# A mixture of experts, computed densely per token before, routed into tiles sorted by expert after

## The reference, cut to what matters

```python
router_logits = x @ wg.T                      # x: layer norm of the residual, 4096 tokens x 128; 8 experts
probs = softmax(router_logits)
topk_w, topk_idx = top_k(probs, 2)
topk_w = topk_w / sum(topk_w)
expert_w = sum(one_hot(topk_idx, 8) * topk_w[..., None], axis=1)
h1 = einsum('th,eih->tei', x, w1)             # 8 experts x 256 inner columns
h3 = einsum('th,eih->tei', x, w3)
y = einsum('tei,ehi->teh', silu(h1) * h3, w2)
out = einsum('te,teh->th', expert_w, y)       # only 2 of the 8 weights of a token are not zero
```

## Time and profile before

| what | value |
|---|---|
| time, median of 3 runs | 1891.29 us (1890.69 to 1895.58) |
| profiled execution, its own time | 1891.74 us |
| its span | 1889.9 us |
| busy: PE, DVE, ACT, POOL | 1677.0, 1390.6, 1243.3, 901.2 us |
| stage A, until the first layer norm of stage B | 0 to 432.1 us |
| stage B, until the first layer norm of stage C | to 808.2 us |
| stage C, until stage D begins | to 1060.3 us |

### The profile page before, as it was taken

The page is one execution under the profiler, slowest core; times in us unless marked ns, Lnnn a source line. Parts: engine busy times, 40 slices in busy tenths (PEclk is TensorE's granted clock), DMA queues, the critical chain, the costliest instruction groups (busy, mean ns, idle before and its releaser), DMA issues.

```text
span 1889.9 us, 38285 instructions
## 1 busy us (share of the span) xinstructions
PE 1677.0 (89%) x12962; PEld 1368.8 (72%) x13024; DVE 1390.6 (74%) x2923; ACT 1243.3 (66%) x2747; POOL 901.2 (48%) x720
## 2 busy tenths in 40 slices
PE   4899999987999999979999599999959699999868
PEld 3777777766766767667777478888847588888746
DVE  6888888865888888866667478888736477777556
ACT  4888888864655555577877377777723377777622
POOL 4666666643544445510101277777700377777500
PEclk9999999998999999989999799999969899999979
DMA  5000000000000000010000000000000000000000
GB/s 203 1 0 0 0 0 0 0 1 1 1 1 1 1 0 0 1 49 1 0 0 0 6 13 15 14 14 15 12 5 1 9 15 14 14 14 14 9 15 34
DMA packets 39787, 23.27 MB, mean 12 GB/s; under 512 B 36257, under 2 KB 36641, under 8 KB 38945
## 3 DMA queue, kind: packets, MB, share of 16 engines
q1 hardware_dynamic: 39712, 22.33, 4.0%
HBM read 11.86 MB, written 2.10 MB: 7 GB/s over the span
## 4 chain that ended last, share of the span: by engine, by line
DVE 35%; ACT 25%; PE 23%; issue 11%; POOL 4%; DMA 1%; DVEq 1%; SPq 0%; POOLq 0%; ACTq 0%
ACT d_p L543 9%; ACT a_p L543 5%; DVE slot L1433 4%; DVE d_ss L1416 4%; DVE d_B L1424 4%; PE slot L367 3%; ACT c_p L543 3%; ACT d_sq L1356 3%; DVE d_A L1422 3%; PE slot L369 3%; PE slot L368 3%; PE slot L1544 2%; DVE b_gl L957 2%; PE slot L771 2%; PE slot L489 2%
## 5 line engine op out<-in xcount | busy, mean ns | idle before, releaser
L1471 POOL TENSOR_TENSOR d_r<-d_vv,nhalf 128x16 f32<-128x16 f32 x64 | 186.4, 2912 | 252.8 <-DVE d_vv L1421 252.8
L998 POOL TENSOR_TENSOR b_sp<-b_s,b_wb 128x512 f32<-128x512 f32 x128 | 170.5, 1335 | 175.3 <-ACT b_s L828 168.8
L665 POOL TENSOR_TENSOR rs<-mv,nhalf 128x1 f32 (+1 forms) x128 | 71.7, 560 | 326.3 <-DVE mv L660 326.3
L543 ACT ACTIVATE d_p<-slot,d_nm,d_r 128x128 f32<-128x128 f32 x512 | 186.0, 469 | 50.8 <-DVE d_nm L1437 50.8
L543 ACT ACTIVATE a_p<-slot,a_nm,a_rq 128x77 f32<-128x77 f32 x512 | 165.4, 454 | 26.2 <-DVE a_nm L567 26.2
L957 DVE TENSOR_TENSOR b_gl<-b_g,b_gh 128x512 fp32r<-128x512 f32 x128 | 133.0, 1039 | 42.4 <-ACT b_gh L832 41.5
L1416 DVE TENSOR_REDUCE d_ss<-d_sq 128x16 f32<-128x1024 f32 x64 | 78.1, 1220 | 109.4 <-ACT d_sq L1356 109.4
L1473 POOL TENSOR_TENSOR d_A<-d_A,d_B 128x1024 f32<-128x1024 f32 x64 | 151.3, 2364 | 0.0
L828 ACT ACTIVATE b_s<-slot 128x512 f32<-128x512 f32 x128 | 76.6, 598 | 81.6 <-PE slot L369 76.7
L543 ACT ACTIVATE c_p<-slot,c_nm 128x77 f32<-128x77 f32 x512 | 118.0, 363 | 11.7 <-DVE c_nm L1156 11.7
L1341 PE MATMUL slot<-d_v,d_pT 128*128 128x65 f32 x1024 | 124.0, 275 | 0.0
(11 more groups left out here) (269 smaller groups left out, 5166.6 us busy)
## 6 DMA issues: line engine op xcount, KB each, us to landing
X<-in_x SPq DMA_DIRECT2D x2, 1024.0 KB, 8.0
d_zx<-Z SPq DMA_DIRECT2D x64, 32.0 KB
H<-Z SPq DMA_DIRECT2D x64, 32.0 KB
out<-f_o SPq DMA_DIRECT2D x8, 256.0 KB, 2.0
d_zx<-Z SPq DMA_DIRECT2D x64, 31.8 KB
H<-Z SPq DMA_DIRECT2D x64, 31.8 KB
stage<-in_wqkv SPq DMA_DIRECT2D x2, 768.0 KB, 5.4
ctx_sb<-in_ctx SPq DMA_DIRECT2D x1, 1232.0 KB, 7.5
```

What stands on the lines that cost most here:

```text
L543: i = e.activation(t["p"][:, h, :], R[slot][:, k // nbank, nk * (k % nbank):nk * (k % nbank) + nk], ACT.Exp, bias=t["nm"][:, h:h + 1], sca ...
L998: e.tensor_tensor(t["sp"][:, c % 2, :], t["s"][:, c % 2, :], t["wb"][:, c // 2 % 2, :], ALU.mult)\
L1471: e.tensor_tensor(t["r"][:, p, :], t["vv"][:, p, :], nhalf[:, 0:16], ALU.pow).then_inc(S("d_r"), 1)
```

## The change

The mixture is computed only for the two experts that a token has. While stage A runs, each finished block is normalised (`r_xn`), its router logits are taken, the two largest are found (`max`, `max_index`), and after every fourth block a place in a list per expert is computed for each token and choice (`chosen`, `places`). POOL scatters the rows to HBM by these places (two indirect transfers of 128 rows per block), into two arrays `xs` that SP first clears (18432 rows of 512 bytes each, 9.44 MB, one of them ahead of `w1e` and `w3e` in the queue). The tokens are in two segments of 16 blocks; tables of each segment (`tables`) say for 40 tiles of 128 rows which expert a tile has. Stage B walks over 80 tiles: SP loads a tile from HBM by an address read from the table, PE transposes it, multiplies it by both weight matrices of one expert (`w13`, 3 passes of 512 columns), transposes the result and multiplies by `w2e`, and SP writes the answer to HBM. Stage C gets two lags more: POOL gathers the two answers of every token (two indirect transfers per block), DVE adds them with their weights to `X` and computes the statistics there. The rest of the diff renames and merges semaphores and passes `part` to the iterations.

The diff, cut to its core:

```diff
@@ load @@
-            for n, src in enumerate((w1e_in, w3e_in, w2e_in)):
-                e.wait_ge(S("split"), (1, 2, 4)[n])
-                e.dma_start(stage[:, n % 2, :], src).then_inc(S(f"stage{n % 2}_in"), 16)
+            nothing = zero[:].unsqueeze(1).to_broadcast([128, ZROWS // 512, 512])
+            for h in range(SEG):
+                if h == 1:
+                    for n, src in enumerate((w1e_in, w3e_in)):
+                        e.wait_ge(S("split"), n + 1)
+                        e.dma_start(stage[:, n, :], src).then_inc(S(f"stage{n}_in"), 16)
+                e.dma_start(xs[h].rearrange(...).rearrange(...), nothing).then_inc(S(f"cleared{h}"), 16)
@@ a_vector, at block b5 = it.b(5) @@
+                    layernorm(e, X, r_["xn"], b5, m).then_inc(S("r_v"), 1)
...
+                    e.tensor_copy(r_["xT"][:], R[1][:, 1, 0:128]).then_inc(S("r_v"), 1)
...
+                    e.max(r_["mx"][:, m, :], R[1][:, 1, 128:128 + NE]).then_inc(S("r_v"), 1)
+                    e.max_index(r_["ix"][:, m, :], r_["mx"][:, m, :], R[1][:, 1, 128:128 + NE]).then_inc(S("r_v"), 1)
+                    if m == 3:
+                        chosen(b5)
+                        places(b5, it.part)
@@ a_pool @@
+        def scatter(e, it, j, lag):
...
+                for k in range(2):
+                    e.indirect_dma_start(xs[it.part][:, :], bass.IndirectOffsetOnAxis(ap=r_["ps"][:, j, k:k + 1], axis=0),
+                                         r_["xn"][:, j, :], None).then_inc(S(f"r_sc{j}"), 16)
+                if it.phase > 0:
+                    scatter(e, it, it.phase - 1, 9)
+                if it.phase == 3:
+                    scatter(e, it, 3, 8)
@@ b_tensor, one tile per iteration @@
+                    e.transpose(bank(m % 2)[:, 0:128], t["x"][:, m, :], ident[:]).then_inc(S("b_T1"), 1)
...
+                    k = e.value_load(table["expert"][0:1, bass.ds(b, 1)], min_val=0, max_val=NE - 1)
...
+                    passes(e, bank(2 + q), [x[:, q, :] for x in t["xT"]],
+                           [w[:, bass.ds(k, 1), :].rearrange("p a b -> p (a b)") for w in w13]).then_inc(S("b_H"), 1)
...
+                    for c in range(2):
+                        mm = e.transpose(bank(4 + q)[:, 128 * c:128 * c + 128], t["g"][:, q, 128 * c:128 * c + 128], ident[:])
...
+                    k = e.value_load(table["expert"][0:1, bass.ds(b, 1)], min_val=0, max_val=NE - 1)
+                    for c in range(2):
+                        mm = e.matmul(bank(6 + q)[:, 0:128], t["gT"][:, q, c, :], w2e[:, bass.ds(2 * k + c, 1), :]...,
+                                      start=(c == 0), stop=(c == 1))
+            pipeline(e, SEG * NT, 4, 4, body)
@@ b_sync, on SP @@
+                    k = e.value_load(table["read"][0:1, bass.ds(b, 1)], min_val=0, max_val=NE * ROOM)
+                    if past(b - 4):
+                        e.wait_ge(S("b_T1"), count(b - 4))
+                    e.dma_start(t["x"][:, m, :], xs[it.part][bass.ds(k, 128), :]).then_inc(S(f"b_x{m}"), 16)
...
+                    e.dma_start(ys[bass.ds(b * 128, 128), :], t["y"][:, m, :]).then_inc(S(f"b_out{m}"), 16)
@@ c_vector, ahead of the maxima @@
+                    for k in range(2):
+                        e.scalar_tensor_tensor(out=rows(X, b), in0=t["yg"][:, m, k:k + 1, :], scalar=r_["w"][:, k, bass.ds(b, 1)],
+                                               in1=rows(X, b), op0=ALU.mult, op1=ALU.add).then_inc(S("c_mix"), 1)
+                    e.bn_stats(st[:, 1, :], rows(X, b)).then_inc(S("c_st"), 1)
+                    e.bn_aggr(agg[:, 1, :], st[:, 1, :]).then_inc(S("c_st"), 1)
+                    e.tensor_tensor(rows(mv, b), agg[:, 1:2, :], eps[:, 1:2, :], ALU.add).then_inc(S("c_st"), 1)
@@ c_pool @@
+                    for k in range(2):
+                        e.indirect_dma_start(c_["yg"][:, m, k, :], None, ys[:, :],
+                                             bass.IndirectOffsetOnAxis(ap=c_["gi"][:, m, k:k + 1], axis=0)).then_inc(S(f"c_g{m}"), 16)
```

More of the change, by code:

```diff
@@ L62, in upto, with pipeline, nth @@
         return last + base + 1
-def pipeline(eng, n, lags, unroll, body):
+def pipeline(eng, n, lags, unroll, body, parts=None, between=None):
     assert lags % unroll == 0 and (n - lags) % unroll == 0
+    ends = (parts or []) + [n]
     for i in range(lags):
[L69 to L72, removed]
+        body(It(i, i % unroll, n, unroll, 0))
+    for part, end in enumerate(ends):
+        first = lags if part == 0 else ends[part - 1]
+        assert (end - first) % unroll == 0
+        if part > 0 and between is not None:
+            between(part - 1)
+        with eng.Fori(first, end - unroll + 1, unroll) as r:
+            for u in range(unroll):
+                body(It(r + u, u, n, unroll, part))
     for i in range(n, n + lags):
-        body(It(i, i % unroll, n, unroll))
+        body(It(i, i % unroll, n, unroll, len(ends) - 1))
+    if between is not None:
+        between(len(ends) - 1)
 def past(b):
     return type(b) is not int or b >= 0
+def nth(n, j, k):
+    return (n - 1) * k + j
 def count(b, j=1, k=1, base=0):
@@ L252, in program @@
         f["o"] = at("f_o", [128, 2, 512])
+        xs = [nc.dram_tensor(f"routed{h}", (ZROWS, D), F32, kind="Internal").ap() for h in range(SEG)]
+        ys = nc.dram_tensor("answers", (SEG * YROWS, D), F32, kind="Internal").ap()
         made = {}
@@ L441, in body @@
                                 e.wait_ge(S("ac_pTb"), it.upto(3))
+                        if half == 1 and b5 is not None:
+                            logits(b5)
                         for k in range(4):
@@ L651, in body @@
                         e.wait_ge(S("rs"), NB // ST)
-            pipeline(e, NB, 4, 4, body)
+            pipeline(e, NB, 8, 4, body, [A_PART], tables)
+            for h in range(SEG):
+                answers(h)
+            e.wait_ge(S("r_ex"), 1)
+            e.tensor_scalar(r_["w"][:, 0, :], r_["dn"][:], 1.0, None, ALU.add).then_inc(S("r_w"), 1)
+            e.wait_ge(S("r_w"), 9)
+            e.reciprocal(r_["w"][:, 0, :], r_["w"][:, 0, :]).then_inc(S("r_w"), 1)
+            e.wait_ge(S("r_w"), 10)
+            e.tensor_tensor(r_["w"][:, 1, :], r_["dn"][:], r_["w"][:, 0, :], ALU.mult).then_inc(S("r_w"), 1)
         def stats_tail(e, b, bn, ag, vs, k=1, j=0, base=0):
@@ L1260, in da_tensor @@
             da_start(e, l)
[L1261 removed]
+            e.wait_ge(S("split"), 8)
             e.wait_ge(S("d_con"), 7)
```

918 lines of the change are left out of this document (487 added, 431 removed).

## The result

The changed kernel takes 2020.62 us (median of 4 runs, 2005.31 to 2023.89) against 1891.93 us before (4 runs, 1890.69 to 1895.58): ratio 1.066, 95% interval 1.060 to 1.072, 129 us slower. The prediction was 1875 us with a range of 1805 to 1960: the wrong side, and outside the range. The profiled execution took 2017.88 us, its span is 2015.8.

What follows compares the result with a forecast made beforehand. PE was taken to bound stage B, rings through DVE and ACT stages A and C. The terms 13 + 55 + 8 + 5 + 9 - 162 + 55 = -17 took 1891.7 to 1875 us, range 1805 to 1960.

Steps and rivals of the forecast that it cites:

- +8 us: Stage A: POOL's indirect transfers mostly hide in slack; 1 us shows in each of eight iterations with four transfers.
- The rival on POOL: POOL becomes stage A's bound at 2.92 us per indirect transfer, giving 1981 us; chance 0.10.
- estimate from the port rule: Stage A: a POOL transfer takes 0.62 us alone, 3.1 beside a VectorE copy; the latter would cost some 120 us.
- 443.9 + 90 = 534 us: Start of stage B: 443.9 us before the change, predicted at 534 with the terms 13, 55, 8, 5 and 9.
- The start's +13: Start of stage A: clearing 9.44 MB ahead of `w1e` and `w3e` in SP's queue stalls everything 13 us.
- Stage B's tile: Stage B: each of 80 tiles takes 2.4 us, bounds 2.1 to 2.8; with the end, -162 us.
- the 2.6 that was named as a sign of being wrong: Stage B: the prediction falls if a tile takes over 2.6 us, where the gain of 17 is used up.
- The term for PE's own work, 1.6: Stage B: PE's transposes, three wide products and two float32 products take 1.6 us per tile.
- The term for the reads, 0.8 for both: Stage B: two table reads at 0.6 us each, partly hidden, between a tile's products on PE.
- reads on the path: Stage B: reads of 0.9 us, PE's sequencer unable to run ahead; tile 3.4 us, kernel 1955; chance 0.19.
- The rival of the low clock: Stage B: at 1.2 GHz PE's 1.6 us becomes 3.1, the tile about 3.3, the kernel 1947; chance 0.08.
- The ring through the maxima: Stage C: maxima, ACT, `c_qTl` and DVE's list form a ring; 1.65 us a block ahead of the maxima adds 55.

Runs made afterwards that it cites:

- e1_xn8: The changed kernel with eight buffers in place of four for `r_xn` and `r_ps`, stage A's loops unrolled by eight: 1918.72 us.
- e7_split: Eight buffers as in e1_xn8, with the second block's two scatters moved behind `a_kn` in POOL's list: 1887.92 us.
- e4_early: The changed kernel with `w1e` and `w3e` loaded ahead of the first clearing in SP's queue: 1984.91 us in one execution.
- e8_read4: e1_xn8 with PE in stage B reading the experts of four tiles by one instruction into four registers: 1920.26 us.
- e6_all: The changed kernel with eight buffers, split scatters, stage C's additions behind the maxima, early `w1e` and `w3e`, and one read per four tiles: 1857.72 us.

## Why the prediction was wrong

*The step that failed* is the one on POOL's scatters, "+8 us". It asked what is queued behind them on POOL, and never what waits for their landing. The scatter reads `r_xn`, `r_xn` has four buffers, and lag 9 against lag 5 is just four blocks: the buffer is wanted in the iteration that sends it off. The numbers were there: `rs`, two issues, a landing of 2 us. The trace shows 4.5 to 4.8 us in 21 iterations, 95.1 us. e1_xn8, which changes only the buffers and the unrolling that they need, gave back 79.5 us before stage B. The four transfers in one iteration were predicted to show 1 us; e7_split gave back 26 us before stage B, in eight iterations, so some 3 each.

*No rival was this one.* The rival on POOL had the place right and the mechanism wrong: it needed 2.92 us per transfer and the rows show 0.96, at most 1.24. Its estimate from the port rule of the Trainium skill (SBUF — State Buffer, SBUF: two separate sides) did not come either: in e1_xn8, where DVE no longer stands while POOL issues, the 64 transfers take 0.95 to 1.32 us, 0.96 in the median. The rule itself is hardly tested by this, for most of DVE's instructions beside them read `slot`, which is PSUM; beside the one layer norm from SBUF, at 293.8 us, a transfer took 1.08.

*Stage A otherwise* was right in its sum. 443.9 + 90 = 534 us for the start of stage B; 531.2 in e7_split. Its parts were a little off both ways: an iteration there takes 14.5 us in the mean, where "near 14" was said (17.6 in the changed kernel). The start's +13 was 11.35 of wait, with the load landing near the predicted 49.9 us; the order of the queue alone makes it, as e4_early shows, and the 394 GB/s taken for the clearing were near what it moved, 409 and 410 from 24 to 40 us.

*Stage B's tile* was 2.70 us, not 2.4, and so past the 2.6 that was named as a sign of being wrong. The term for PE's own work, 1.6, was right (1.48 to 1.58). The term for the reads, 0.8 for both, measures 1.1; a read takes 0.30, some 0.17 of register work stands behind each, and what makes up the remaining 0.1 to 0.2 of a tile is not shown. So 24 us were missed there, and 7 more on the way to stage C. The rival "reads on the path" was right in that the reads stand on PE's path (taking them out shortens the tile by more than their own length); that PE's sequencer cannot run ahead over its waits is not shown by itself, and the price of 0.9 a read is too high. SP did not bound the tile, at 0.33 and 0.36 us a transfer, but its list with the writes was next: 1.93. The rival of the low clock did not come in the changed kernel, where stage B ran at 1.00 in the window of 660 to 840 us; it came in e8_read4 and e6_all, behind gaps of 2.4 us.

*Stage C* took 9.13 us in a block at the full clock against 9.0 predicted, and 307.0 us in e7_split against 311. The ring through the maxima, the reason given, is shown in part: out of 1.65 us a block put ahead of them, moving them behind gave 0.45 back.

*The clock* was in no term. In stage A it rose from 0.85 to 0.90 and 0.92 (100 to 400 us; e1_xn8, e7_split) as the waits went, and the windows named above show it fall where PE stood: behind the wait for `r_xn` in stage A, behind the gap of the bulk reads in stage B. So the 80 us of the wait hold both the standing and the slower products behind it; the runs do not part them. Stage C is another matter. It took 322.5 us at 0.83 (over the whole stage) in the profiled execution of the changed kernel, and 304 to 318 us at 0.88 to 0.95 in eight kernels with the same instructions there, so 5 to 18 us go with the clock. Why it differs from one execution to the next stays open.

Together, in the profiled execution: 103 us in stage A (80 of wait and 26 of POOL's list, less the 3 by which the rest was better than said), 31 in stage B, 12 in stage C, less 3 behind it: 143 on top of 1875.

## What to carry to other kernels

Where a change gives a buffer a new reader that is a transfer, compare the lag of the reader's issue with the lag of the next writer: if the difference is the number of buffers, the writer waits in the same iteration for issue and landing, and everything behind it in its list too. When work is added to an engine with slack, look at the fullest iteration, not at the mean: it was the iteration with four transfers that cost, and moving two of them behind `a_kn` cured it. Count the reads of registers on a matrix engine's list, and the register work that comes with each: reading a value once, keeping it and leaving that work out was worth 53 us here, second only to the wait. And when work is gathered into one long gap, look at the granted clock behind the gap before judging it: here it hid that the reads had become cheaper.

## What the hardware showed that was not expected

- An indirect transfer of 128 rows of 512 bytes, scatter or gather, holds POOL 0.96 to 0.99 us in the median with 0.30 between two, lands 2.2 (scatter) and 2.5 us (gather) after its issue, and a scatter is hardly longer where DVE works beside it (e1_xn8: 954 to 1315 ns over 64).
- A read of one value from SBUF into a register takes 0.30 us on PE and 0.27 on SP, but four values in one read take 1.00. With the register work and the addresses that come with them, the two reads of a tile cost PE's list 1.1 us.
- PE stood 2.4 us at each head of e8_read4's loop, and the granted clock behind the gap was 0.50 (650 to 652 us), then 1.00 again (653 to 658 us); a tile took 3.05 us there and 1.49 later.
- SP's transfers with an address from a register took 0.33 to 0.36 us here, where the nearest rows of before had 0.55 and 0.66.
- The clearing of HBM, 9.44 MB from one small tile, and the loads beside it moved 396 GB/s (window 16 to 24 us), and 409 and 410 GB/s in the next two windows of 8 us.
